# Second stage of a fused pair of attentions on one core: VectorE's slots reordered, GpSimd's additions held, one turn of keys moved behind a score

## The reference

```python
att = softmax(q @ k.T / 4) @ v          # 16 heads, of batch 0 alone
x = x + att[0]                          # tgt2, added to every batch
norm_X = layernorm(ctx) * norm1_w + norm1_b
norm_F_L = layernorm(x) * norm2_w + norm2_b
attended = softmax(norm_F_L @ norm_X.T / 16) @ norm_X
h = gelu(attended @ fc1_w.T + fc1_b)
cross = h @ fc2_w.T + fc2_b
norm_cross = layernorm(cross) * norm3_w + norm3_b
self_att = softmax(norm_cross @ norm_cross.T / 16) @ norm_cross
out = norm_F_L + gamma2 * (cross + gamma1 * self_att)
```

## Time and profile before

| | |
|---|---|
| median of 3 runs | 238.79 us (237.54 to 243.37) |
| profiled execution | 239.72 us |
| its span, first to last instruction | 237.9 us |
| mean granted TensorE clock | 0.964 |
| TensorE busy | 211.2 us (89%) |
| VectorE busy | 183.0 us (77%) |
| ScalarE busy | 151.0 us (63%) |
| GpSimd busy | 144.3 us (61%) |

### The profile page before, as it was taken

How to read it: one execution, slowest core, us unless ns; L and a number is a source line. 1 busy time by engine, 2 the same in 40 slices (tenths; PEclk the granted TensorE clock), 3 DMA queues, 4 the chain that set the end, 5 groups by cost and what they waited for, 6 DMA issues and landing times.

```text
span 237.9 us, 4947 instructions
## 1 busy us (share of the span) xinstructions
PE 211.2 (89%) x1730; PEld 152.1 (64%) x1730; DVE 183.0 (77%) x355; ACT 151.0 (63%) x292; POOL 144.3 (61%) x232
## 2 busy tenths in 40 slices
PE   8999979897789999999999899999997499899750
PEld 8775646685656879778797686877683154445220
DVE  6599968689979987878779999961254665988773
ACT  2177847454358859778596996866497346777520
POOL 6547551477499999879985983900038888222330
PEclk9999999999999999999999999999999956999995
DMA  7980000075352445525455000000000003364458
GB/s 239 392 298 4 1 4 0 7 245 164 117 176 55 165 138 178 171 70 155 140 176 175 4 0 1 4 0 1 3 0 3 0 34 145 115 237 182 176 209 325
DMA packets 14712, 26.81 MB, mean 113 GB/s; under 512 B 1760, under 2 KB 1760, under 8 KB 14688
## 3 DMA queue, kind: packets, MB, share of 16 engines
q1 hardware_dynamic: 14400, 25.98, 31.6%
q10 hardware_dynamic: 288, 0.52, 0.7%
HBM read 18.11 MB, written 8.39 MB: 111 GB/s over the span
## 4 chain that ended last, share of the span: by engine, by line
PE 62%; DVE 18%; ACT 7%; POOL 7%; issue 4%; DVEq 0%; ACTq 0%; POOLq 0%
PE psum L1087 18%; PE psum L1024 10%; PE psum L1095 5%; PE psum L972 4%; DVE xN L379 3%; DVE bn L359 3%; PE psum L1125 3%; PE psum L1207 2%; PE psum L1107 2%; DVE Fall L594 2%; DVE hmax L397 2%; PE psum L1240 2%; PE psum L1175 2%; DVE nmax L523 2%; PE psum L1194 2%
## 5 line engine op out<-in xcount | busy, mean ns | idle before, releaser
L1087 PE MATMUL psum<-XT,Fall 128*128 128x256 f32 x256 | 61.0, 381 | 1.7 <-ACT Fall L861 1.7
L1087 PEld LDWEIGHTS psum<-XT,Fall 128*128 128x128 f32 x256 | 46.1, 190 | 7.3 <-ACT Fall L861 2.3
L699 POOL TENSOR_SCALAR cN<-cN,nmean,rstd 128x256 f32<-128x256 f32 x64 | 37.3, 594 | 2.5 <-POOL rstd L686 2.1
L679 POOL TENSOR_TENSOR xN<-xN,tgt 128x512 f32<-128x512 f32 x28 | 35.6, 1277 | 4.8 <-DVE xN L379 4.8
L686 POOL TENSOR_TENSOR rstd<-vps,minus_half 128x8 f32<-128x8 f32 (+1 forms) x16 | 24.2, 1512 | 19.9 <-DVE vps L370 19.6
L884 ACT ACTIVATE PT<-psum 128x512 f32<-128x512 f32 x32 | 19.1, 598 | 24.3 <-PE psum L1095 24.2
L891 ACT ACTIVATE E<-psum,nmax 128x256 f32<-128x256 f32 x64 | 26.7, 473 | 11.9 <-DVE nmax L523 11.9
L523 DVE TENSOR_REDUCE nmax<-psum 128x2 f32<-128x512 f32 x32 | 22.0, 687 | 15.2 <-PE psum L1087 14.7
L379 DVE TENSOR_SCALAR xN<-xN,bn,rstd 128x256 f32<-128x256 f32 x64 | 32.7, 557 | 0.5 <-POOL rstd L686 0.4
L579 DVE TENSOR_REDUCE nm<-psum 128x4 bf16<-128x1024 f32 x16 | 19.5, 1221 | 11.9 <-PE psum L1175 11.8
L858 ACT ACTIVATE XT<-psum,b1s,w1s 128x512 f32<-128x512 f32 x32 | 23.0, 793 | 4.0 <-PE psum L1024 4.0
(11 more groups left out here) (175 smaller groups left out, 348.1 us busy)
## 6 DMA issues: line engine op xcount, KB each, us to landing
cN<-ctx SPq DMA_DIRECT2D x32, 256.0 KB, 3.0
xN<-x SPq DMA_DIRECT2D x32, 256.0 KB, 4.2
out<-Fall SPq DMA_DIRECT2D x32, 256.0 KB, 2.3
x0T<-x0t ACTq DMA_DIRECT2D x1, 256.0 KB, 2.8
c0T<-c0t ACTq DMA_DIRECT2D x1, 256.0 KB, 4.0
wqT<-wqt SPq DMA_DIRECT2D x1, 256.0 KB, 3.8
wkT<-wkt SPq DMA_DIRECT2D x1, 256.0 KB, 4.2
wvT<-wvt SPq DMA_DIRECT2D x1, 256.0 KB, 4.4
```

The costliest lines, as they stand in the source:

```text
L679: pool.tensor_tensor(xN[:, b % SLOTS, :], xN[:, b % SLOTS, :], tgt2[:, :, :].rearrange("p t d -> p (t d)"), ALU.add).then_inc(y_ok, 1)
L699: pool.tensor_scalar(own, own, nmean[:, p % 4, NT * m + t:NT * m + t + 1], root_of(p, 0, m, t), ALU.add, ALU.mult)\
L1087: last = pe.matmul(bank[SBANK1[b % 3]][:, t * N:(t + 1) * N], Fall[:, b, c, t * P:(t + 1) * P], XT[:, p % 4, c, m * N:(m + 1) * N], start= ...
```

## The change

Only the order of instructions and three waits change; no instruction is added or taken away.

- **VectorE, slots 1 to 11.** x's statistics of batch 7 and the variances of pair 3 move from the end of slot 1 behind the first statistics of batch 8 in slot 2; x's statistics of batch 8, `normal(6)` and `normal(7)` move from slot 2 to slot 3, and what slot 3 did (both statistics of batch 9, the variances of pair 4) stands around the maximum of slot 4. From there to slot 11 the statistics, variances and normals are dealt out anew around the maxima: `normal(8)` and `normal(9)` both stand in slot 5 (they were in 4 and 5), `normal(10)` and `normal(11)` in slot 7 (6 and 7), `normal(12)` and `normal(13)` in slot 9 (8 and 9). Variances 5 stands in slot 6 behind the maximum (it was in 5), variances 6 in slot 8 (7), variances 7 in slot 10 (9). From slot 12 on the order is the old one.
- **GpSimd.** `add(7)` waits until `normal(5)` is done on VectorE, `add(9)` until `normal(7)` is, as `add(5)` already waits for `normal(3)`. In slots 4 and 6 both normals of a pair (8 and 9, 10 and 11) follow the root directly; the second of them stood behind the next slot's addition.
- **TensorE, slot 6.** The keys of pair 4 (the fifth pair) are turned behind `score(6)` instead of ahead of it.

```diff
--- before.py
+++ after.py
@@ -539,7 +539,30 @@
 
         for b in range(B):
             k, m, q = b // 2, b % 2, b // 4
-            if b >= 4 and k + 3 < PAIRS:
+            if b == 4:
+                statistics(9, 0)
+            elif b == 6:
+                statistics(11, 0)
+            elif b == 7:
+                statistics(12, 0)
+                statistics(12, 1)
+            elif b == 8:
+                statistics(13, 0)
+                statistics(13, 1)
+                variances(6)
+            elif b == 9:
+                statistics(14, 1)
+                statistics(15, 0)
+            elif b == 10:
+                statistics(15, 1)
+                variances(7)
+                statistics(16, 0)
+            elif b == 11:
+                statistics(16, 1)
+                statistics(17, 0)
+                statistics(17, 1)
+                variances(8)
+            elif b >= 12 and k + 3 < PAIRS:
                 statistics(b + 6, 0)
                 statistics(b + 6, 1)
                 if m == 1:
@@ -556,17 +579,37 @@
                 statistics(6, 1)
                 normal(4)
                 normal(5)
+            elif b == 2:
+                statistics(8, 0)
                 statistics(7, 1)
                 variances(3)
-            elif b == 2:
-                statistics(8, 0)
+            elif b == 3:
                 statistics(8, 1)
                 normal(6)
                 normal(7)
-            elif b == 3:
-                statistics(9, 0)
+            elif b == 4:
                 statistics(9, 1)
                 variances(4)
+            elif b == 5:
+                statistics(10, 0)
+                normal(8)
+                normal(9)
+                statistics(10, 1)
+            elif b == 6:
+                statistics(11, 1)
+                variances(5)
+            elif b == 7:
+                normal(10)
+                normal(11)
+            elif b == 8:
+                statistics(14, 0)
+            elif b == 9:
+                normal(12)
+                normal(13)
+            elif b == 10:
+                normal(14)
+            elif b == 11:
+                normal(15)
             elif k + 2 < PAIRS:
                 normal(b + 4)
             for part in LATE.get(b, ()):
@@ -674,8 +717,8 @@
             if b == 4:
                 pool.wait_ge(tgt2_ok, 2 * NT)
                 pool.wait_ge(zy_ok, 4)
-            if b == 5:
-                pool.wait_ge(zy_ok, 8)
+            if b in (5, 7, 9):
+                pool.wait_ge(zy_ok, 2 * b - 2)
             pool.tensor_tensor(xN[:, b % SLOTS, :], xN[:, b % SLOTS, :], tgt2[:, :, :].rearrange("p t d -> p (t d)"),
                                ALU.add).then_inc(y_ok, 1)
 
@@ -717,7 +760,10 @@
                 add(b + 6)
             if m == 0 and k + 2 < PAIRS:
                 root(k + 2)
-            if EARLY <= k + 2 < PAIRS:
+            if b in (4, 6):
+                normal(b + 4)
+                normal(b + 5)
+            elif b >= 8 and k + 2 < PAIRS:
                 normal(b + 4)
 
         sums, roots = [0], [0]
@@ -1243,10 +1289,12 @@
 
         for b in range(B + 1):
             k, m, q = b // 2, b % 2, b // 4
-            if k + 1 < PAIRS and (m == 1 or k + 1 >= EARLY):
+            if k + 1 < PAIRS and (m == 1 or k + 1 >= EARLY) and b != 6:
                 turned(k + 1, m)
             if b < B:
                 score(b)
+            if b == 6:
+                turned(k + 1, m)
             if b % 4 == 1 and 1 <= q < QUADS:
                 project(q)
             if b % 4 == 2:
```

## The result

| | before | after |
|---|---|---|
| median, same chip | 238.86 us (4 runs, 237.54 to 243.37) | 241.18 us (4 runs, 240.46 to 242.62) |
| ratio, 95% interval | | 1.0084 (1.0056 to 1.0113) |
| profiled execution, its span | 239.72, 237.9 us | 241.01, 239.2 us |
| mean granted TensorE clock | 0.964 | 0.957 |

So the change costs between nothing and some 2 us; it doesn't give the 1.6 us of the forecast. Ratios leave out runs more than 1.5% above their kernel's fastest, so that a ratio can lie under what its two medians give.

A forecast was written before the change was run, and what follows sets the result against it. TensorE bounds the kernel, GpSimd nearly as tight. Holds and reorder give 4.0 us, less 1.0 at pair 5's keys and 1.4 at pair 6's: 1.6 gained, 238.79 to 237.2 us; range 234.8 to 240.2.

The forecast's parts named there:

- What bounds the kernel, and the ceiling: TensorE is busy 89% of the span; its 4.50 us idle between 52.9 and 77.2 cap the gain.
- Slots 0 to 5: Held additions free VectorE's normals: score 5 starts at 60.6, 3.7 us earlier, but pair 4's root only 0.8 earlier.
- Slot 6: Score 6 goes ahead of the keys' turn, starts at 63.9, 6.0 us earlier; TensorE's gain reaches 4.0.
- Slots 6 to 8: One half of VectorE's normals 10 and 11 is shut out by an addition, end 76.0; score 8 gains 3.0 us.
- rival 1: Slots 7 and 8: additions shut out two VectorE halves; gain 0.3 to 0.7 us, 238.3 us; chance 0.20.
- Slot 12 on, and later: The old orders return, TensorE is last again, and slot 11's gain is carried if every engine follows TensorE.
- Rival 4: Slot 22: VectorE's algebra beside its slots, with GpSimd waiting, eats TensorE's lead; 238.8 us; chance 0.06.
- rival 3: GpSimd becomes the bound as no half passes between additions 13 and 14; 239.9 to 240.3 us; chance 0.12.
- Rival 5: Its place and claim are cut from the text; the only rival not within 4.8 us of no change; chance 0.05.

The follow-up runs named there:

- e2: The changed kernel with VectorE's normals 10 and 11 ahead of maximum 7 instead of behind it: 237.87 us, ratio 0.9966.
- e5: The changed kernel with ten filling products on TensorE ahead of pair 6's keys in slot 10: 241.25 us, ratio 0.9969.
- e10: The changed kernel with fifteen filling products in TensorE's third-stage wait for GpSimd: 239.49 us, ratio 1.0031.
- e11: The changed kernel run once more with nothing altered, in a later dozen runs: 239.56 us, ratio 1.0016.
- e13: The changed kernel with ten filling products ahead of pair 6's keys and fifteen in the third stage: 238.11 us, ratio 0.989.
- e6: The changed kernel with VectorE's normals 10 to 13 ahead of their maxima and GpSimd's normals 12 and 13 together: 236.89 us, ratio 0.9876.
- e8: The changed kernel with GpSimd's normals 10 and 11 apart again, addition 13 between them as before: 239.14 us, ratio 1.0007.
- e7: The changed kernel without the moved turn, pair 4's keys turned ahead of score 6 again: 243.65 us, ratio 1.0162.
- e14: The kernel before with VectorE's new order alone, no holds, context normals apart, keys ahead of score 6: 246.01 us, ratio 1.0272.
- e3: The kernel before with only the turn of pair 4's keys moved behind score 6: 241.73 us, ratio 0.9993.
- e4: The kernel before with only additions 7 and 9 held behind normals 5 and 7: 241.03 us, ratio 1.0061.

## Why the prediction was wrong, step by step

*What bounds the kernel, and the ceiling*: right. 4.50 us of idle time became 1.35 in these four windows.

*Slots 0 to 5*: right to 0.2. Less 0.65, score 3 starts at 55.29 (55.4 said), score 4 at 57.45 (57.5), score 5 at 60.57 (60.6), R4 at 62.62 (62.8).

*Slot 6*: score 6 at 63.86 (63.9). K8 and K9 with N8 and N9 beside them were the term with the widest bounds, 66.8 to 68.0 for K9's end, 67.4 taken. It was 66.96: four context halves took 2.52 against 2.16 alone (65.09 and 72.08 in the fences above), 0.36 more. The eight halves of both engines were all done 2.7 us after the first began, where 1.36 and 2.16 one behind the other are 3.5, so these two operations ran side by side in part. A half that met an addition was held up by more: N10's second, beside A13, took 1.36 us, where a free one takes 0.41 (each of the four from 43.75 in before).

*Slots 6 to 8, the step that failed*: "I take one half shut out: end 76.0". GpSimd ran 0.5 to 0.7 ahead of my replay (R5 69.61 against 70.1, K11's end 73.59 against 74.3), since its halves were cheaper. I counted that as the good side of my bounds. It was the bad one: N10 stood behind maximum 7, whose time TensorE sets (73.03), so an earlier GpSimd meant that A13 came upon the second half already, and A14 upon the third. The first half didn't pass freely either: it met K11's last half and took 0.71 us. This is read from the rows; no run moves GpSimd alone.

```profile
74.31 1.36 DVE L379 TENSOR_SCALAR xN<-xN,bn,rstd 128x256 f32<-128x256 f32 x1
```

Two halves were shut out by additions, as in rival 1; the end was 76.6. Score 8 was 3.8 us ahead of before (3.0 forecast), which made the wait at pair 6's keys longer and not shorter. R6 started at 78.18 (77.3 forecast, 78.5 in rival 1), K13 ended at 83.63 (83.0 and 84.2). Score 10 was 0.95 us ahead of before, and not 1.6: between my forecast and rival 1, which had 0.3 to 0.7. e2 shows that the place of N10 and N11 is the cause: with these normals elsewhere R6 had only the usual 0.18 us of idle time ahead.

*The step that was missing, and that turned the gain into a loss*: TensorE's clock in the slots. The replay took all its durations from rows at a clock of 1.00 and had no term for a fall. The forecast itself had TensorE waiting 1.6 us at pair 6's keys, a wait that before didn't have. It came as 0.39 and 2.03, the clock fell to 0.50 for 3.4 us, and 1.63 us went with it: 0.95 less 1.63 is the -0.68 of the stretch. e5 shows this: with the wait filled and nothing else changed, the stretch is 46.24. It holds for the stretch, in three profiles with the wait as it is (after, e10, e11) and two with it filled and no longer (e5, e13); in the medians, which lie up to 1.6 us apart for the same kernel, it can't be told from the third stage's clock.

*Slot 12 on, and later*: right for this change, whose 0.68 of loss at pair 7's keys is 0.53 at the end of the second stage. The gain of e5 is carried whole, those of e6 and e8 in part. The stretch's 0.68 and the start's 0.65 give 1.33, and the two profiled executions differ by 1.29. Rival 4 is out: the 0.92 of e5 are not eaten by slot 22. The third stage doesn't only move along, and the forecast has no term for its clock: in the profiles without its filler a clock of 0.50 lasted 6.8, 10.2 or 17.1 us there, and pair 7's keys to the end took 144.4 to 145.0, 145.5 to 145.8, and 145.8 to 148.0 us with them.

*The range* (234.8 to 240.2): the second set of the changed kernel, 239.56, lies in it, the first, 241.18, does not. Its upper end came from rival 3, which priced a late GpSimd at full clock. Rival 5, the one below the range, is out: the lowest of the sixteen runs of the changed kernel took 237.82 us (e11). Rival 3 has a slip too: K13 ended 5.7 us behind R6 in the forecast and in rival 1, which gives 85.4 and not 85.6. Of the 4.0 us between the forecast of 237.2 and the first median, the slots explain 2.3 (1.6 of gain forecast, 0.68 of loss measured); the rest lies in the start, in the third stage and in which runs a median of four takes in, and can't be divided among them.

## What to carry to other kernels

Freeing one engine moves the place where two others meet: replay the two engines that shut each other out to their next meeting, and ask of each bound which side is the bad one there. Try VectorE's short instructions beside GpSimd's short ones, not beside its long ones; here, with halves of 0.41 us beside halves of 0.55 and not beside additions of 1.27, that was worth 3.2 us of the stretch, half of it through the clock (e2 against after). Where an edit gathers small waits of TensorE into one, price the products behind it at half clock too (here a score took 2.97 us in place of 1.89, behind waits of 0.39 and 2.03), and fill the wait if it can't be moved.

## What the runs showed of the hardware

Four halves of VectorE's `tensor_scalar` (128x256, float32) took 1.36 to 1.39 us with GpSimd idle, and 1.71 to 1.95 beside four of GpSimd's own `tensor_scalar` halves. They took 1.90 when they met the last 0.46 us of an addition (128x512; e2, at 80.75), 2.19 to 2.75 when they met one addition in other places, most often with context halves beside it, and 2.59 to 3.60 when they met two. Of two additions back to back each held up one half (1.24 and 1.35 us before, 1.36 and 1.35 after); the next half ran in 0.40, as one of four does with GpSimd idle (0.41).

TensorE's granted clock went from 1.00 to 0.50 for 3.4 us, behind waits of 0.39 and 2.03 us within 2.4 us of each other (after, e10, e11), of 1.98 and 0.60 (e7), of 1.15 and 1.88 (e14, 0.14 us before the second ended), and behind a single wait of 2.03 (e7, at 86.66). It stayed at 1.00 behind single waits of 1.98 (e8, at 74.86), of 1.73 (e3, at 71.96), and of 2.03 (e14, at 81.38), and behind one of 1.80 that another of 0.40 followed (e4, at 69.22 and 72.22). Products of no use in the wait, ten in 2.40 us, kept it at 1.00 (e5, e13). Why 2.03 us was harmless in one place and not in the other isn't settled.
